# Attention mask added by VectorE in a fused sum-and-minimum that writes the score bank back, instead of by mask products on TensorE; queries negated

## The reference, cut to what matters

```python
q = (inputs @ Wq + bq).reshape(bs, n, 8, 32)      # inputs = layernorm(x); k and v alike
logits = jnp.einsum('bqhd,bkhd->bhqk', q, k) / np.sqrt(HEAD_DIM)
mask = (adj > 0)[:, None, :, :]
logits = jnp.where(mask, logits, NEG_INF)
attn = jax.nn.softmax(logits, axis=-1)
out = jnp.einsum('bhqk,bkhd->bqhd', attn, v).reshape(bs, n, EMBED_DIM)
x = x + relu(out @ Wo + bo)
```

## Time and profile before

| | |
|---|---|
| median of 3 runs | 2882.18 us (2881.75 to 2882.73) |
| profiled execution | 2882.74 us, of which the span of the trace is 2880.8 us |
| PE, DVE, ACT, POOL busy, whole span | 92%, 70%, 67%, 56% |
| attention phase | from the start to about 603 us |
| PE, DVE, ACT, POOL busy, 300 to 400 us | 98.4, 80.7, 65.7, 71.6 us of 100 |
| granted TensorE clock, 300 to 400 us | 1.00 |

### The profile page before, as it was taken

The page is one execution under the profiler, slowest core; times in us unless marked ns, Lnnn a source line. Parts: engine busy times, 40 slices in busy tenths (PEclk is TensorE's granted clock), DMA queues, the critical chain, the costliest instruction groups (busy, mean ns, idle before and its releaser), DMA issues. The chain is left out here.

```text
span 2880.8 us, 117560 instructions
## 1 busy us (share of the span) xinstructions
PE 2645.6 (92%) x44480; PEld 2411.5 (84%) x44480; DVE 2012.6 (70%) x6103; ACT 1924.5 (67%) x5044; POOL 1620.0 (56%) x2677
## 2 busy tenths in 40 slices
PE   7999999978888888869999999999999999999956
PEld 5777777767777777759999999999999999999955
DVE  6887788844444444447777777877777888888868
ACT  4666666644444444437888888788787778888734
POOL 6777777610000000016888885666666677777755
PEclk9999999999999999989999999999999999999989
DMA  3111111000000000020000011100000100000003
GB/s 92 38 39 38 39 37 37 22 8 13 13 13 13 13 13 13 13 78 25 25 26 25 25 36 45 32 9 9 9 9 8 34 26 9 9 9 9 8 8 109
DMA packets 110837, 74.60 MB, mean 26 GB/s; under 512 B 51504, under 2 KB 109360, under 8 KB 110512
## 3 DMA queue, kind: packets, MB, share of 16 engines
q1 hardware_dynamic: 96800, 61.03, 7.3%
q10 hardware_dynamic: 13968, 12.72, 1.5%
HBM read 51.68 MB, written 22.02 MB: 26 GB/s over the span
## 5 line engine op out<-in xcount | busy, mean ns | idle before, releaser
L1637 PE MATMUL g_H<-g_hT_upper,g_w_upper 128*128 128x256 f32 x1536 | 461.4, 300 | 0.2
L1637 PE MATMUL g_H<-g_hT_upper,g_w_rest 128*128 128x256 f32 x1536 | 434.9, 283 | 0.0
L1637 PE MATMUL g_H<-g_hT_rest,g_w_upper 128*128 128x256 f32 x1536 | 434.6, 283 | 0.0
L1665 PE MATMUL g_F<-g_w_upper,g_act_upper 128*128 128x256 f32 x1408 | 410.3, 291 | 8.2 <-DVE g_act_rest L1405 4.9
L1190 ACT ACTIVATE g_act_raw<-g_H,g_small 128x256 f32<-128x256 f32 x768 | 319.5, 471 | 124.6 <-PE g_H L1637 123.5
L762 POOL COPY l_xt<-seq 128x64 f32 x256 | 60.5, 236 | 599.6 <-PE l_O L773 595.9
L1665 PE MATMUL g_F<-g_w_upper,g_act_rest 128*128 128x256 f32 x1408 | 395.8, 281 | 0.0
L1665 PE MATMUL g_F<-g_w_rest,g_act_upper 128*128 128x256 f32 x1408 | 395.1, 281 | 0.0
L330 ACT ACTIVATE a_probs<-a_S,a_nmax 128x256 f32<-128x256 f32 x512 | 236.7, 480 | 120.8 <-DVE a_nmax L424 87.9
L1405 DVE TENSOR_TENSOR g_act_rest<-g_act_raw,g_act_upper 128x512 fp32r<-128x512 f32 x352 | 267.9, 762 | 46.1 <-ACT g_act_upper L1195 40.5
L801 ACT ACTIVATE l_ic<-l_G 128x128 f32<-128x128 f32 x256 | 71.1, 278 | 342.4 <-PE l_G L773 342.4
(11 more groups left out here) (224 smaller groups left out, 8305.2 us busy)
## 6 DMA issues: line engine op xcount, KB each, us to landing
gmask<-masks ACTq DMA_DIRECT2D x97, 128.0 KB, 2.0
x<-in_x_dram SPq DMA_DIRECT2D x32, 256.0 KB, 3.1
a_adj<-in_adj_dram SPq DMA_DIRECT2D x32, 256.0 KB, 2.7
hidden<-l_hs SPq DMA_DIRECT2D x512, 16.0 KB, 1.4
seq<-hidden SPq DMA_DIRECT2D x32, 256.0 KB, 2.7
out_dram<-q_res SPq DMA_DIRECT2D x32, 256.0 KB, 2.1
masks<-gmask SPq DMA_DIRECT2D x32, 128.0 KB, 1.7
g_w_raw<-in_L_gnn_W_dram SPq DMA_DIRECT2D x6, 512.0 KB, 3.9
```

The costliest lines, as they stand in the source:

```text
L1637: last = pe.matmul(hidden_bank[m // 2][:, m % 2 * N:(m % 2 + 1) * N], w[:, c, m * P:(m + 1) * P], x[:, c, :], start=(c == 0 and k == 0), s ...
L1665: last = pe.matmul(ff_bank[:, it * D:(it + 1) * D], x[:, m, it * P:(it + 1) * P], w[:, m, :], start=(m == 0 and it == 0 and k == 0), stop= ...
```

## The change

The eight `cover` products of a graph are gone, and `scores` starts each region of a bank anew instead of adding to it. `qscale` and the bias of the queries carry a minus sign, so that the banks hold the negated scores. The mask is 0 or +1e30. `largest` is now two instructions per head, one for each half of the rows: bank = bank + mask, written back into the bank, with the minimum of the row as accumulated output, which goes to `nmax` by an accumulator read. The exponential takes the bank with scale -1. The wait for the mask moves from PE (ahead of `cover` of head 0) to DVE (ahead of `largest` of head 0), and POOL makes the next mask once `max_done` says that the old one was read, not `scores_ps`.

```diff
 def masks(b, i):
-    after(pool, scores_ps, (b - 1) * H)
+    after(pool, max_done, (b - 1) * H)
     alone(pool, adj_in, b * 16 + 16, pool_passed)
-    pool.tensor_scalar(mask[i][:, :], adj[:, :, :].rearrange("p t n -> p (t n)"), 0.0, MASKED,
+    pool.tensor_scalar(mask[i][:, :], adj[:, :, :].rearrange("p t n -> p (t n)"), 0.0, -MASKED,
...
-        last = act.activation(probs[h % PROBS][:, it, :], score_bank[h % HG][:, it * N:(it + 1) * N],
-                              ACT.Exp, bias=nmax[:, h, it:it + 1], accum_out=den[:, h, it:it + 1])
+        last = act.activation(probs[h % PROBS][:, it, :], score_bank[h % HG][:, it * N:(it + 1) * N], ACT.Exp,
+                              scale=-1.0, bias=nmax[:, h, it:it + 1], accum_out=den[:, h, it:it + 1])
...
-def largest(b, h):
-    dve.wait_ge(scores_ps, b * H + h + 1)
-    dve.tensor_reduce(nmax[:, h, :], score_bank[h % HG][:, :].rearrange("p (t k) -> p t k", t=NT), AX.X,
-                      ALU.max, negate=True).then_inc(max_done, 1)
+def largest(b, h, i):
+    if h == 0:
+        dve.wait_ge(mask_done, b + 1)
+    alone(dve, scores_ps, b * H + h + 1, passed)
+    for it in range(NT):
+        part = slice(it * N, (it + 1) * N)
+        last = dve.tensor_tensor_reduce(out=score_bank[h % HG][:, part], in0=score_bank[h % HG][:, part],
+                                        in1=mask[i][:, part], scale=1.0, scalar=3.0e38,
+                                        op0=ALU.add, op1=ALU.min, accum_out=nmax[:, h, it:it + 1])
+    last.then_inc(max_done, 1)
...
-dve.memset(qscale[:, :], HD ** -0.5)
-dve.tensor_scalar(bqs_col[:, :], bq_col[:, :], HD ** -0.5, None, ALU.mult).then_inc(bqs_done, 1)
+dve.memset(qscale[:, :], -HD ** -0.5)
+dve.tensor_scalar(bqs_col[:, :], bq_col[:, :], -HD ** -0.5, None, ALU.mult).then_inc(bqs_done, 1)
...
-def cover(b, h, i):
-    if h == 0:
-        pe.wait_ge(mask_done, b + 1)
-    pe.matmul(score_bank[h % HG][:, :], t.identb[:, :], mask[i][:, :], start=True, stop=False, skip_group_check=True)
...
-                             kT[o:o + HD, g, :], start=False, stop=True, skip_group_check=True)
+                             kT[o:o + HD, g, :], start=True, stop=True)
```

More of the change, by code:

```diff
@@ L480, in graph @@
                     for h in range(HG):
-                        largest(b, h)
+                        largest(b, h, i)
                     early_out(b, 0)
@@ L660, in graph @@
                         turn_probs(b, h)
-                        cover(b, h + HG, i)
                     values(b)
                     turn_probs(b, 2)
-                    cover(b, 2 + HG, i)
                     if exists(b - 2):
@@ L669, in graph @@
                     turn_probs(b, 3)
-                    cover(b, 3 + HG, i)
                     scores(b, 1)
@@ L676, in graph @@
                         if exists(b + 1):
-                            cover(b + 1, j, 1 - i)
                             if j == 0:
@@ L686, in _ @@
                 keys(0)
-                for j in range(HG):
-                    cover(0, j, 0)
                 walk(pe, graph)
```

## The result

The changed kernel takes 2900.55 us (median of 4 runs, 2900.32 to 2901.31), beside 2881.99 us for the kernel before (median of 4, one run more than the three shown above): a ratio of 1.0064, interval 1.0047 to 1.0082. It is 0.6% slower where 0.4% faster was forecast. The number lies inside the stated range, at its upper edge; the sign is wrong. It came out on rival D's side, though not by D's row alone.

A forecast was written before the change was run, and what follows sets the result against it. PE, 98% busy, was not taken as the sole bound, since it waits for v_out on DVE's queue. Per graph +0.12 - 0.22 - 0.25 = -0.35 us, over 31 periods -10.9 us, gave 2871 us; range 2863 to 2902.

The forecast's parts named there:

- rival D: DVE's queue, steps 2 and 5: the write-back lengthens pitch p to 0.79; +14 us, 2896; chance 0.20.
- pitch p: DVE's time per head for the two fused instructions, reads included: 0.686 us forecast, against 0.60 for the reduce.
- step 2: `largest` of head 0 to v_out, DVE's queue, 5.48 us; forecast +0.12 us a graph.
- step 5: scores(b,1) to the next k_out, 8.06 us; forecast -0.25 us: 0.15 up to q_out and 0.10 behind it.
- step 1: k_out to `largest` of head 0, 1.98 us, DVE's own queue; forecast no change.
- the prediction's own formula: Change of a graph by pitch p: 4p - 2.62 - 0.47, beyond 0.70 another 4p - 2.79; zero at 0.735.
- step 3: v_out to turn_xn, 0.82 us, where PE waits 0.18 us for v_out; forecast no change.
- rival B: PE is the bound and the time of all eight covers is won: 55 us, 2827; chance 0.04.
- step 4: turn_xn to scores(b,1), 1.21 us, PE's queue; one cover gone, forecast -0.22 us.
- q: Distance from the scores of heads 4 to 7 to q_out, inside step 5; forecast from 5.29 to 5.14 us.
- C: Write to PSUM costs a little (Trainium skill's access-overhead rule points here), pitch p about 0.72: -4 us, 2878; chance 0.20.
- F: DVE's longer loop costs 0.4 us at each turn or 0.05 at each head: sum -5 to about 0; chance 0.02.

The follow-up runs named there:

- e2: The kernel before with its eight mask products deleted and nothing else, so the scores stay unmasked; 2872.42 us, ratio 0.9970.
- e6: The changed kernel plus probe groups of four fused or plain sums between PSUM and SBUF at the attention phase's start; 2921.60 us, one run, probe included.
- e7: The kernel before with the reduce's wait made a separate wait and semaphore increment ahead of it; 2890.14 us, ratio 1.0025.
- e1: The changed kernel with the fused sum written to SBUF instead of the score bank, and the exponential reading it there; 2890.46 us, ratio 1.0028.

## Why the prediction was wrong, point by point

Three terms of the sum were wrong, and each made the forecast too fast: the pitch p in steps 2 and 5, the "nothing" for the new waits in steps 1 and 5, and the gain of step 5. The first alone turns the sign by the prediction's own formula.

- **That PE's busy share is no bound** was right: PE waits for v_out, as step 3 said, and the 55 us of rival B are not there (e2). The four covers ahead of turn_xn gained nothing (steps 1 and 2 are 2.23 and 5.45 in e2, 2.23 and 5.46 before); step 4 measured -0.22 as forecast.
- **The pitch of the fused instruction** was mis-sized: p = 0.765, not 0.686. What failed first is the reason given for taking L1330's row: that source memory doesn't matter was extended to the destination. For a plain sum that is right (e6), for one with an accumulator read it isn't. By my own formula p = 0.765 makes +0.24 a graph, +7 us. Four heads make 0.32 us of it in step 2; the measured step is +0.40 where +0.12 stood.
- **Step 1, "nothing", and the 1.16 us kept in step 5** failed next. They measured +0.15 and +0.16: "the new waits cost nothing" looked at whether the semaphore is there in time, and not at the instructions that the wait is made of. e7 shows 0.18 of the 0.31. The order of the changed kernel didn't show them as separate rows, but the change's `alone` did.
- **Step 5's gain** on PE, -0.15 and then -0.10, failed too: with the reduce in place (e2) q moved by 0.05 and the rest of the step hardly at all. The limit that I missed is `project` behind ScalarE's copy into `seq`, 0.22 us, which the cover had hidden. In the changed kernel q isn't set by this but by DVE's queue: 5.55 where 5.09 was put, 0.16 of it the late start and 0.29 the pitch. PE's side was off as well, since turn_probs 4 came 0.34 us later and not at most 0.05. The -0.10 for a cover that "still ran" had no row behind it: q_out to k_out is 2.77 us in either kernel.
- Added up: forecast -0.35, missed +0.15 (step 1), +0.28 (step 2) and +0.48 (step 5: +0.40 in q, +0.08 behind it), measured +0.56.
- **The signs named beforehand**: step 4 and the missing waits ahead of early_out 0 and q_out came as said. The pitch of 0.38 was the sign against the forecast, and the period without a loop's turn is 18.08 us where 17.2 was said. PE's wait for v_out is 0.57, not 0.8, and DVE's busy share 84%, not 86%, since the period itself is longer.
- **The rivals**: D had the place, the sign and the kind of cause right, and its time of 2896 was 4.5 us short, because it too took the other steps from the forecast. Its reason, one bank read and written at once, is refuted by e6. C's range of p ended at 0.755, just short of the 0.765 measured, and the rule that it leaned on would by the prediction's own formula (p = 0.725) have left a gain of 2.5 us, not the 4 given. F priced a cost ahead of the waits at 0.05 for each head; it is about 0.15 at the first head of a half and hidden at the others, and 0.02 was too small a chance for something that the diff shows.

## What to carry to other kernels

When an engine's work is made smaller, follow its queue to the next place where it waits for someone else: all that is won ahead of that place is given back there, and what the removed work had been hiding (here a wait of 0.22 us for ScalarE) becomes visible behind it. A move of work to a second engine that has 20% idle is priced by where that engine's queue is waited for, not by its idle share; here moving two statistics out of such a stretch gave as much as deleting all eight mask products did. And price an instruction as it stands in the program, with its accumulator read and with the instructions of its wait.

## What the runs showed of the hardware

- An accumulator read behind a fused VectorE sum and minimum that wrote to PSUM takes 0.14 us, and the pitch of 128x256 is 0.38, except at the first of a group (0.35); behind one that wrote to SBUF they are 0.08 and 0.34 (e6, e1). A plain sum has 0.336 for both destinations, in place, to another bank or to SBUF (e6).
- A wait with a semaphore increment of its own ahead of VectorE's reduce delays it by 0.06 us, against a wait attached to it, where DVE came from other work without idle time, and by 0.12 where DVE stood waiting (e7).
- Exponentials of 128x256 with an accumulated sum follow one another every 0.49 us out of SBUF and every 0.45 out of PSUM (e1, before).
